# Two attention stages on one core: the engines' loops over batches and over unit pairs written out as straight code

## The reference

```python
xn = _layernorm(x, axis=-1)
s = _L0_attn_ref(xn, L0_attn_W_qkv, L0_attn_W_o)      # 16 heads of 16, alibi bias, causal softmax
g = _silu(_L0_ffn_ref(xn, L0_ffn_W1, L0_ffn_W2, L0_ffn_W3))   # 256 -> 1024 -> 256, Hadamard transform inside
x = x + s * g
xn = _layernorm(x, axis=-1)
s = _L1_attn_ref(xn, wq, wk, wv, wo, q_norm_w, k_norm_w, rope_cos, rope_sin)  # 16 heads of 128, causal
g = _silu(_L1_ffn_ref(xn, ...))   # a shared expert and 16 routed experts, the 4 best of each row
x = x + s * g
```

## The kernel before

| engine | line | runs over | body | passes |
|---|---|---|---|---|
| TensorE | L670 | batches 1 to 6 | 2 batches | 3 |
| ScalarE | L1057 | batches 1 to 6 | 2 batches | 3 |
| VectorE | L1508 | batches 2 to 6 | 1 batch | 5 |
| TensorE | L901 | steps 16 to 63 | 16 steps | 3 |
| ScalarE | L1209 | steps 16 to 47 | 16 steps | 2 |
| VectorE | L1719 | steps 16 to 47 | 16 steps | 2 |
| GpSimd | L1861 | steps 16 to 63 | 16 steps | 3 |

## Time and profile before

### The profile page before, as it was taken

How to read it: one execution, slowest core, us unless ns; L and a number is a source line. 1 busy time by engine, 2 the same in 40 slices (tenths; PEclk the granted TensorE clock), 3 DMA queues, 4 the chain that set the end, 5 groups by cost and what they waited for, 6 DMA issues and landing times.

```text
span 1408.8 us, 26582 instructions
## 1 busy us (share of the span) xinstructions
PE 1272.3 (90%) x9326; PEld 1107.9 (79%) x9327; DVE 846.9 (60%) x1731; ACT 597.1 (42%) x1351; POOL 473.7 (34%) x488
## 2 busy tenths in 40 slices
PE   5699979979998879989897899899999999999996
PEld 4588878768777766667666888889998999898996
DVE  4647547557556553333346777767665676667685
ACT  3333323323323334444453444454554555455542
POOL 0112332332331320000007878644343444343442
PEclk9799999999999999999999999999999999999998
DMA  5744314223101943323223121200000000000001
GB/s 196 282 177 154 134 59 150 100 97 143 46 31 36 340 174 94 93 82 97 89 76 116 53 76 46 75 1 31 2 1 31 1 31 1 1 1 1 1 24 38
DMA packets 63658, 112.07 MB, mean 80 GB/s; under 512 B 6977, under 2 KB 36033, under 8 KB 62017
## 3 DMA queue, kind: packets, MB, share of 16 engines
q1 hardware_dynamic: 57408, 93.79, 19.0%
q0 software_dynamic: 6144, 16.79, 3.6%
HBM read 49.86 MB, written 60.69 MB: 78 GB/s over the span
## 4 chain that ended last, share of the span: by engine, by line
PE 80%; DVE 8%; issue 7%; ACT 3%; POOL 1%; DMA 1%; another core or an unknown queue 1%; SPq 0%; ACTq 0%; DVEq 0%; POOLq 0%
PE bank L705 7%; PE six L722 6%; PE six L830 4%; PE bank L792 4%; PE bank L794 4%; PE bank L793 4%; PE bank L392 4%; PE bank L393 3%; PE bank L394 3%; PE bank L867 2%; PE bank L865 2%; PE bank L866 2%; PE bank L804 2%; PE six L844 2%; PE bank L805 2%
## 5 line engine op out<-in xcount | busy, mean ns | idle before, releaser
L1822 POOL TENSOR_TENSOR rstd<-msq,half_pow 128x8 f32<-128x8 f32 x64 | 105.5, 1648 | 163.1 <-DVE msq L1633 162.7
L1149 ACT ACTIVATE pT<-six,rstd 128x256 f32<-128x256 f32 x128 | 60.9, 476 | 213.6 <-PE six L831 213.6
L1759 POOL TENSOR_TENSOR hid_l<-hid,hid_h 128x256 fp32r<-128x256 f32 x64 | 48.2, 753 | 243.4 <-ACT hid_h L963 243.4
L1834 POOL TENSOR_TENSOR pT<-pT,tri_mul 128x512 f32<-128x512 f32 x64 | 84.3, 1318 | 130.8 <-ACT pT L1195 129.9
L1233 DVE TENSOR_TENSOR yT1l<-six,yT1h 128x512 fp32r<-128x512 f32 x64 | 44.3, 692 | 135.0 <-ACT yT1h L1200 135.0
L705 PE MATMUL bank<-experts,xT 128*128 x316 | 109.5, 470 | 17.5 <-issue 16.8
L1626 DVE TENSOR_TENSOR sq<-xs 128x512 f32<-128x512 f32 x128 | 102.1, 797 | 23.3 <-ACT xs L1168 23.3
L792 PE MATMUL bank<-bw_h,xT1h 128*128 128x512 f32 x256 | 106.9, 418 | 6.5 <-issue 6.5
L794 PE MATMUL bank<-bw_l,xT1h 128*128 128x512 f32 x256 | 101.8, 398 | 0.0
L793 PE MATMUL bank<-bw_h,xT1l 128*128 128x512 f32 x256 | 101.1, 395 | 0.0
L830 PE MATMUL six<-qT,kT 128*128 128x256 f32 x256 | 78.5, 388 | 18.7 <-issue 15.4
(11 more groups left out here) (282 smaller groups left out, 4068.4 us busy)
## 6 DMA issues: line engine op xcount, KB each, us to landing
cells_scratch<-zeros SPq DMA_DIRECT2D x8, 4352.0 KB, 14.9
xg<-cells_scratch SPq DMA_DIRECT2D x79, 128.0 KB, 2.0
cells_scratch<-y SPq DMA_DIRECT2D x79, 128.0 KB, 1.7
experts<-pack_experts_dram SPq DMA_DIRECT2D x16, 608.0 KB
raw<-pack_attn_dram SPq DMA_DIRECT2D x8, 1024.0 KB, 4.9
raw<-pack_w_dram SPq DMA_DIRECT2D x2, 1024.0 KB, 4.8
xT_scratch<-xT1h_c SPq DMA_DIRECT2D x8, 256.0 KB, 2.0
xT_scratch<-xT1l_c SPq DMA_DIRECT2D x8, 256.0 KB, 2.6
```

What stands on the lines that cost most here:

```text
L1822: pool.tensor_tensor(out=rstd[:, r, :], in0=msq[:, r, :], in1=half_pow[:], op=ALU.pow).then_inc(rstd_sb, 1)
L1834: pool.tensor_tensor(out=p, in0=p, in1=tri_mul[:].unsqueeze(1).unsqueeze(1).to_broadcast([P, 2, 2, P]), op=ALU.mult).then_inc(masked1, 1)
```

## The change

Seven hardware loops become loops of the program that writes the code, so their bodies are emitted once for each pass with plain numbers in the place of registers. The order of the instructions on each engine, the tiles, the transfers and the semaphores stay as they are.

```diff
@@ TensorE
             batch(0, 0, True, False)
-            with pe.Fori(0, NB // 2 - 1) as w:
+            for w in range(0, NB // 2 - 1):
                 batch(2 * w + 1, 1, False, False)
                 batch(2 * w + 2, 0, False, False)
             batch(NB - 1, 1, False, True)
...
             unit_pair(0, True)
-            with pe.Fori(1, NU // 2) as w:
+            for w in range(1, NU // 2):
                 unit_pair(w, False)
@@ ScalarE
-            with act.Fori(0, NB // 2 - 1) as w:
+            for w in range(0, NB // 2 - 1):
...
-            with act.Fori(1, NU // 2 - 1) as w:
+            for w in range(1, NU // 2 - 1):
                 unit_pair(w, False, False)
@@ VectorE
-            with dve.Fori(2, NB - 1) as b:
+            for b in range(2, NB - 1):
                 batch(b, False, False)
...
-            with dve.Fori(1, NU // 2 - 1) as w:
+            for w in range(1, NU // 2 - 1):
                 unit_pair(w, False, False)
@@ GpSimd
-            with pool.Fori(1, NU // 2) as w:
+            for w in range(1, NU // 2):
                 unit_pair(w, False)
```

## The result

The changed kernel takes 1363.54 us (median of 4 runs, 1362.57 to 1363.95) against 1377.95 for the kernel before (4 runs, 1373.42 to 1381.57). The ratio is 0.9897 with a 95% interval of 0.9864 to 0.993: 1.03% faster, where 1363.6 us and 17.5 us less than 1381.1 were forecast.

What follows compares the result with a forecast made beforehand. The kernel was taken as nearly TensorE-bound (busy 1272.3 of 1408.8 us), losing time at long loop edges. First attention 8.02 plus second 9.46 gave 17.5 us, so 1381.1 to 1363.6 us, range 1353 to 1374.

Steps and rivals of the forecast that it cites:

- TensorE's long branches are the whole of it: Loop edges at L670 and L901: dear only on TensorE with long bodies, 3.3 to 3.7 us per taken branch.
- Second attention, 9.46 us: TensorE's two L901 edges: 4.86 + 4.60 us saved; lower bound 5.75 us, the idle pieces alone.
- the idle piece: TensorE's idle time at a second-attention edge, 3.00 us at the first and 2.75 at the second, to vanish.
- 1.6 us of low clock: Step behind a second-attention edge: partly at 1.2 GHz, 11.18 us against 9.59, 1.59 more, to vanish.
- First attention, 8.02 us: TensorE's two L670 edges: batches behind them 3.97 and 4.05 us longer than the next, all to be saved.
- VectorE's loop, bounds 50.62 and +1.11 us: First-attention batches: 50.62 us each (15.88 us gain) or 1.11 us worse each (gain 3.58); no change taken.
- "The middle": Value taken between the two bounds for VectorE's loop in the first attention: no change, leaving 8.02 us.
- Rivals B and C: First-attention batches: B fast form, 50.62 us each, 1355.8 us, chance 0.13; C slow form of batch 7, 1368.1, chance 0.12.
- Register work, at most 0.3 us per batch: Sequencer's computing of wait values in loops: at most 3.6 us over both attentions; nothing taken.
- The 27.7 us between span and median: Whole kernel: profiled span 1408.8 us against timed median 1381.1, difference taken as the profiler's and unchanged.
- Rival A: Removed edges: branches cheap, something else stands there; change worth 1.3 us, time 1379.8, chance 0.08.
- Rival D: Expert loop L773: moved code makes its seven edges dear, 4.7 us each, up to 1396.5 us; chance 0.04.

Runs made afterwards that it cites:

- tensor_only: Kernel before with only TensorE's two loops (L670, L901) written out, the other engines' five kept: 1361.61 us, ratio 0.9875.
- others_only: Kernel before with the five loops of ScalarE, VectorE and GpSimd written out, TensorE's two kept: 1382.49 us, ratio 1.0016.
- second_only: Kernel before with only the four loops over unit pairs of the second attention written out: 1392.86 us, ratio 0.9942.
- one_edge: Changed kernel with TensorE's unit pairs 2 and 3 a loop again, one taken branch: 1389.57 us, ratio 0.9928 to the kernel before.
- before_again: The kernel before, unchanged, run again on the third chip: 1409.1 us, ratio 1.001.
- first_only: Kernel before with only the three loops over the batches of the first attention written out: 1395.92 us, ratio 0.996.
- hinted: Kernel before with all seven loops kept, TensorE's two given a back-edge hint; its long branches took 221 to 377 ns (whole time not given).
- short_bodies: Changed kernel with steps 2 to 5 of units from 2 on as short two-pass TensorE loops: 1359.29 us, ratio 0.9839 to the kernel before.

## Why the prediction was right

*TensorE's long branches are the whole of it.* Right. tensor_only has all the gain, others_only none, and no long branch is left in the changed kernel.

*Second attention, 9.46 us.* Right in mechanism, at the top in size. Against the first trace, the two steps came out 4.87 us shorter, as worked out. second_only measured 8.1 us (4.6 to 11.6). Of the two terms the idle piece (2.7 to 3.0 us) is there each time. The 1.6 us of low clock is not: one_edge and before_again show edges with the clock at 1.00. The step should have read "about 3 or 4.8 us each". One reading in it was loose: of the 4.86 us the prediction called all but the idle piece the clock, but 3.00 and 1.59 leave 0.27 us, and before_again has the same 0.27 (3.31 us longer for 3.04 idle) with the clock at 1.00. It belongs to the edge.

*First attention, 8.02 us.* Right. others_only shows 5.6 and 4.0 us where nothing else disturbs the batches. first_only measured 5.6 us (1.7 to 9.5), on a chip where the heads of the batches are held up anyway; that such a hold absorbs part of the edge is argued, and the traces of that chip point the same way: the stretch from the first to the sixth store of the slots takes 260.3 us with the two edges (second_only) and 257.0 (first_only) or 258.9 (one_edge) without, where others_only and the changed kernel lie 10.0 us apart (247.8 and 237.7).

*VectorE's loop, bounds 50.62 and +1.11 us.* The value taken, nothing, was right, and the reasons were not. "The middle" of a gain of 15.88 us and a loss of 4.44 would have been a gain of 5.7, so no change was a choice and not their middle. I treated the differences between batches as forms of the code. They come with the hold at the heads of batches, and so with the chip or the moment: 47.5 us in one trace of the changed kernel and, between slots, 50 to 53 in another. Neither bound was one, and a batch went to 47.5. It did no harm since kernels on the same chip share it. Rivals B and C were thus badly put, as their tell-tales (50.6, 53.7) could come true with no bearing on the change.

*Register work, at most 0.3 us per batch.* Right. With VectorE's and ScalarE's loops kept and TensorE's written out, a batch from slots to slots in tensor_only is

```profile
227.83 0.17 DVE L1392 CAST slots_all<-r_slot 128x8 f32 x1
...
275.59 0.17 DVE L1392 CAST slots_all<-r_slot 128x8 f32 x1
```

47.76 us against 47.56 in the changed kernel, 0.2 us. hinted keeps the register work on every engine, TensorE's too, and its batch takes

```profile
228.26 0.17 DVE L1392 CAST slots_all<-r_slot 128x8 f32 x1
...
276.11 0.17 DVE L1392 CAST slots_all<-r_slot 128x8 f32 x1
```

47.85 us, 0.3 us above the changed kernel.

*The 27.7 us between span and median, put down to the profiler.* Wrong. The changed kernel's profiled run has a span of 1360.7 us and its own time was 1362.57, beside 1363.3 to 1363.95 for its other runs: profiling adds nothing that can be seen. others_only keeps TensorE's loops on a chip without the holds, and its span is 1381.5 us. It opens the expert loop at 498.4 us, the first trace at 530.7, 32.3 later (its line is below); in the expert loop the first trace is 5.0 us shorter, as its clock fell in fewer groups; behind it the two are equal. So the 27.7 us are the holds less some clock, in an execution that wasn't like the timed runs. Taking them as unchanged kept the forecast sound, but 17.5 us was read from it.

```profile
L773 PEldq MOVE  x1: 34/34/34, 498.4 to 498.4; - x1
```

*Rival A* (branches cheap or inflated by the profiler) falls with tensor_only and hinted. The figure of about 108 ns that the prediction takes there from the Trainium skill ("Advanced Engine Details and Errata", section Control Flow Timing) agrees with the short bodies only within a factor of about two: the medians are 45, 56 and 208 ns. *Rival D* (the expert loop's edges become dear) falls with L773 at 215 ns.

The rule of the Trainium skill ("Runtime: NRT & Kernel Launch", section Instruction fetch mechanics), that a taken branch to code no longer held waits for its fetch, agrees with hinted and short_bodies: the same branch falls from 3.3 us and more to 0.2 to 0.4 us when the code is asked for early, and stays under 0.3 us when the body is short.

That the median came out within 0.1 us of the forecast is luck. It was reckoned from a median that was 3 us above that of the next measurement, and the terms were each good to some 3 us.

## What to carry to other kernels

Look up the loop-closing branches of each engine in the trace before judging a loop. Here 40 to 260 ns was the edge itself, and over 3 us stood only at the end of TensorE's long bodies (946 matmuls or more; bodies of up to some 140 were cheap, and nothing between was tried). There a prefetch hint at the head of the body was as good as straight code within the scatter of the runs, and it keeps the program small. Price an idle piece on TensorE with the clock behind it, in rows, and look at more than one execution: in the expert stage 0.6 us less idle time gave 0.6 us per group where the clock had held, and 2.3 us where it had fallen.

## What the hardware showed that I had not expected

- The granted clock behind an idle piece of about 3 us fell in some executions and not in others (0.85 or 1.00 over the next step), for the same code. In the expert groups with pieces of 1.98 us it fell in 70 of 84 (0.93 over the group), and with 1.36 in none.
- While GpSimd issues eight indirect transfers (10 us), ScalarE begins on TensorE's last scores 0.46 or 4.31 us after TensorE began them, depending on chip or moment. The changed kernel took 1363.54 us where its trace is without these holds and 1388.65 where it has them. What holds them up wasn't found; a kernel without the sends wasn't tried.
- Chips differ by 2% on the same kernel (1379.03, 1400.06 and 1406.27 us), more than the change is worth.
